# Second attention of a two-layer kernel: both maximum fills of a head ahead of the value product on TensorE

## What is computed

```python
mixed_q = hidden_states @ wq + bq
mixed_k = hidden_states @ wk + bk
mixed_v = hidden_states @ wv + bv
...                                   # P and Z, one pair for each query and head
G = -(j[None, None, None, :] - P[..., None]) ** 2 * 2.0 / Z[..., None] ** 2
scores = jnp.einsum('bhqd,bhkd->bhqk', q, k) / jnp.sqrt(jnp.float32(D))
scores = scores + G
probs = jax.nn.softmax(scores, axis=-1)
ctx = jnp.einsum('bhqk,bhkd->bhqd', probs, v)
...
return ctx @ wo + bo
```

## Time and profile before

| | us |
|---|---|
| median of 3 runs | 1796.94 |
| lowest and highest | 1796.51, 1797.92 |
| profiled execution | 1798.3 |
| span from its first to its last instruction | 1796.6 |
| first fill for the maxima starts | 1046.3 |
| last fill starts | 1726.2 |
| last scores of the stage start | 1772.1 |

### The profile page before, as it was taken

How to read it: one execution, slowest core, us unless ns; L and a number is a source line. 1 busy time by engine, 2 the same in 40 slices (tenths; PEclk the granted TensorE clock), 3 DMA queues, 4 the chain that set the end, 5 groups by cost and what they waited for, 6 DMA issues and landing times.

```text
span 1796.6 us, 27707 instructions
## 1 busy us (share of the span) xinstructions
PE 1649.1 (92%) x10488; PEld 492.0 (27%) x10488; DVE 1277.0 (71%) x2570; ACT 965.8 (54%) x1109; POOL 670.0 (37%) x408
## 2 busy tenths in 40 slices
PE   7999999999999999995999769999999999999995
PEld 3232323333333323322444311111111111111122
DVE  6767576666667575722233489999999999999974
ACT  2444545444444444442343315777777777777774
POOL 4577877878887878892000110000000000000012
PEclk8999999999999999997999857999999999999998
DMA  4100000000000000001012440111211121111000
GB/s 112 35 9 13 14 13 9 12 13 10 16 7 19 8 16 10 13 13 31 2 36 58 100 94 1 24 24 24 41 24 31 31 46 26 24 23 24 2 2 24
DMA packets 76215, 46.40 MB, mean 26 GB/s; under 512 B 22158, under 2 KB 74930, under 8 KB 76082
## 3 DMA queue, kind: packets, MB, share of 16 engines
q1 hardware_dynamic: 74738, 43.38, 11.4%
q10 hardware_dynamic: 1344, 1.25, 0.2%
HBM read 25.66 MB, written 9.31 MB: 19 GB/s over the span
## 4 chain that ended last, share of the span: by engine, by line
PE 29%; DVE 17%; ACT 3%; DMA 2%; issue 1%; SPq 1%; POOL 0%; DVEq 0%; ACTq 0%; POOLq 0%
DVE maxpart L1717 15%; PE ps_o L1613 9%; PE ps_h L1013 6%; PE ps_r L1575 5%; ACT probs L1534 3%; PE ps_e L1603 2%; DMA qrows<-maxrow 2%; PE ps_g L995 1%; PE ps_u L1000 1%; PE ps_u L1022 1%; PE ps_r L1592 1%; SPq L1456 0%; PE ps_g L1091 0%; PE ps_r L1658 0%; PE ps_j L1044 0%
## 5 line engine op out<-in xcount | busy, mean ns | idle before, releaser
L1717 DVE TENSOR_REDUCE maxpart<-ps_r 128x1 f32<-128x512 f32 x1024 | 634.5, 682 | 26.8 <-PE ps_r L1575 25.9
L1534 ACT ACTIVATE probs<-ps_e 128x1024 f32<-128x1024 f32 x512 | 504.7, 1023 | 194.9 <-PE ps_e L1603 189.8
L328 POOL TENSOR_TENSOR acc<-acc,probs 128x1024 f32<-128x1024 f32 (+3 forms) x256 | 502.9, 1964 | 77.9 <-ACT probs L362 55.3
L362 ACT ACTIVATE probs<-ps_e 128x1024 f32<-128x1024 f32 (+1 forms) x320 | 285.7, 901 | 380.7 <-DVE ps_e L697 131.0
L1575 PE MATMUL ps_r<-krows,qrows 60*128 60x512 bf16 x1024 | 346.9, 402 | 50.8 <-DVE maxpart L1717 17.9
L528 PE MATMUL ps_o<-probs,v 128*64 128x512 f32 (+3 forms) x1280 | 308.6, 561 | 0.2 <-ACT pv_raw L369 0.2
L618 DVE TENSOR_REDUCE maxpart<-ps_x 128x2 f32<-128x1024 f32 x192 | 234.5, 1222 | 75.3 <-PE ps_x L443 75.3
L1603 PE MATMUL ps_e<-qrows,krows 62*128 62x512 bf16 x1024 | 278.8, 386 | 4.2 <-DMA qrows<-maxrow 3.3
L1613 PE MATMUL ps_o<-probs,v 128*9 128x512 f32 x2048 | 269.2, 598 | 12.4 <-ACT probs L1534 12.3
L1499 POOL TENSOR_TENSOR rstd<-veps,power 128x4 f32<-128x4 f32 x8 | 8.1, 1014 | 700.2 <-DVE veps L1767 700.2
L1575 PEld LDWEIGHTS ps_r<-krows,qrows 60*128 60x128 bf16 x1024 | 80.0, 94 | 466.2 <-DVE maxpart L1717 340.4
(11 more groups left out here) (258 smaller groups left out, 1368.6 us busy)
## 6 DMA issues: line engine op xcount, KB each, us to landing
qrows<-q_rows SPq DMA_DIRECT2D x64, 192.0 KB
rbc<-rden SPq DMA_DIRECT2D x128, 64.0 KB, 2.1
q_rows<-parts_q SPq DMA_DIRECT2D x24, 128.0 KB, 2.4
k_rows<-parts_k SPq DMA_DIRECT2D x24, 128.0 KB, 2.4
krows<-k_rows SPq DMA_DIRECT2D x16, 192.0 KB, 5.9
w_rows<-parts_w SPq DMA_DIRECT2D x6, 256.0 KB, 2.6
qrows<-a_rows SPq DMA_DIRECT2D x64, 24.0 KB
qrows<-w_rows SPq DMA_DIRECT2D x64, 24.0 KB
```

The source lines that it names most:

```text
L328: pool.tensor_tensor(acc[:, u % 2, :, o:], acc[:, u % 2, :, o:], probs[:, turn % RING, :, o:], ALU.add)\
L362: act.activation(probs[:, turn % RING, :, o:], ps_e[:, turn % 2, :, o:], ACT.Exp, scale=1.0 / math.sqrt(D0))\
L1534: act.activation(probs[:, HG * (turn % 2) + hh], ps_e[:, e % 2], ACT.Exp).then_inc(s_ex, 1)
L1717: dve.reduce_max(maxpart[:, at:at + 1], ps_r[:, k, :], AX.X).then_inc(s_bf[k], 1)
```

## The change

The first two ring operations that are left in `rest` are now issued together between the scores and the value product of a head. Before, the first stood ahead of the value product and the second behind it. Heads without a value product issue the same as before.

```diff
@@ -1668,13 +1668,11 @@
                 rest, late = list(ops), turn % TU == 1
                 for hh in range(HG):
                     scores(turn, hh)
-                    for op in rest[:1]:
+                    for op in rest[:2]:
                         ring(op)
+                    rest = rest[2:]
                     if hh % 2 == late and turn > 0:
                         pv(turn - 1, hh // 2)
-                    for op in rest[1:2]:
-                        ring(op)
-                    rest = rest[2:]
                     if turn >= (NU - 1) * TU and (turn % TU, hh) in PE_SLOT:
                         step(*PE_SLOT[turn % TU, hh])
                 for op in rest:
```

## The result

The changed kernel takes 1824.82 us (median of 4 runs, 1823.66 to 1825.24) against 1797.26 for the kernel before in runs beside it (1796.51 to 1797.92). The ratio is 1.0152, with a 95% interval of 1.0135 to 1.017: slower by 27.6 us. The forecast was 1823.5.

The account below looks back on a forecast made before the run. The bound was taken as a TensorE-VectorE loop through a three-bank ring, not VectorE's busy time. Per unit 1.76 + 0.29 - 0.25 = +1.8 us, over 14.75 units +26.6: 1796.94 becomes 1823.5 us, range 1813 to 1832.

Parts of the forecast that it names:

- short interval: Steady turn, between value products, through the first fill behind one: scores now come first, 2.47 us becomes 2.69, +0.22.
- long interval: Steady turn's other gap between value products: stays 2.69 us, but set by fills waiting for reduces instead of by ScalarE.
- rest of a unit: Intervals of a unit (eight key-tile turns) outside the steady pattern, walked singly; whole unit +1.8 us.
- waits for the placed maxima: Interval between value products set by the load of the maxima: 3.29 us before and after, 0.
- six fills: Interval with six fills between value products, on the fill loop: +0.22 us.
- output turn: Interval where the second fill ahead of the second value product needs the transposes' bank: 2.65 to 2.94 us, +0.29.
- five fills: Interval with five fills between value products, on the fill loop: +0.22 us.
- maxima turn: Turn with the transposed maxima, whose first value product now waits for a reduce: 3.03 to 2.78 us, -0.25.
- rule against the row: TensorE: the row-group rule would free a slot by pairing fills; a trace row shows it already shared, so no gain.
- Faster: Rival: pairing takes TensorE out of the loop, turns fall to 4.8 us, 1753 us in all; chance 0.06.
- No change: Rival: the 0.22 us meets slack at the first fill in every short interval, 1797 us; chance 0.05.
- Slower still: Rival: the exponential's path, value product to scores to exponential, does not shorten, 13 us more, 1837 us; chance 0.05.

Follow-up runs that it names:

- experiments at one value product only: Kernel before, with the new order at only one of a turn's two value products: at the first only 1796.41 us, at the second only 1831.65 us.
- swapped fill: Changed kernel, first fill of a head following a value product placed between the two scores matmuls, which also change places: 1799.35 us, ratio 1.002.
- value product first: Against the kernel before, the value product stands directly behind its head's scores and both fills behind it: 1828.32 us, ratio 1.0174.
- late value products: Value products at heads 1 and 3 in turns 3 to 6 too: in the kernel before 1785.76 us, in the changed kernel 1816.41 us.
- fill between the scores: Changed kernel, first fill of a head following a value product placed between the two scores matmuls, these in usual order: 1821.01 us, ratio 1.0141.
- new order at the second value product: Kernel before, with both fills ahead of only the second of a turn's two value products: 1831.65 us, ratio 1.0194.

## Why the prediction was right

**The bound.** Read as a loop of two engines rather than by the busy shares. The experiments at one value product only bear this out: the same instructions with only their places changed take 1796 or 1832 us.

**The short interval, +0.22.** Predicted 2.69, measured 2.68 to 2.69. That the step between the scores and the first fill is its cause is shown by the swapped fill, which takes that step away and brings the short interval back to 2.48, and by the value product first, which puts scores on the other side of the loop and has steady turns as long, 5.39.

**The long interval, unchanged.** Predicted to change its owner from ScalarE to the fill loop at the same length. The late value products show both sides: 2.69 falls to 2.47 in the kernel before and stays 2.69 in the changed one.

**The rest of a unit.** The value products of the changed kernel, the view of the earlier trace rows:

```profile
1400.83 1.04 PE L1613 MATMUL ps_o<-probs,v 128*9 128x512 f32 x8
1404.11 1.04 PE L1613 MATMUL ps_o<-probs,v 128*9 128x512 f32 x8
1406.79 1.04 PE L1613 MATMUL ps_o<-probs,v 128*9 128x512 f32 x8
1410.67 1.05 PE L1613 MATMUL ps_o<-probs,v 128*9 128x512 f32 x8
...
1414.88 1.05 PE L1613 MATMUL ps_o<-probs,v 128*9 128x512 f32 x8
1417.83 1.05 PE L1613 MATMUL ps_o<-probs,v 128*9 128x512 f32 x8
1421.11 1.05 PE L1613 MATMUL ps_o<-probs,v 128*9 128x512 f32 x8
...
1442.59 1.04 PE L1613 MATMUL ps_o<-probs,v 128*9 128x512 f32 x8
1445.37 1.05 PE L1613 MATMUL ps_o<-probs,v 128*9 128x512 f32 x8
```

| interval | before | predicted | after |
|---|---|---|---|
| waits for the placed maxima | 3.29 | 3.29 | 3.28 |
| six fills | 3.66 | 3.88 | 3.88 |
| output turn | 2.65 | 2.94 | 2.95 |
| five fills | 3.06 | 3.28 | 3.28 |
| maxima turn | 3.03 | 2.78 | 2.78 |
| unit | 42.79 | 44.6 | 44.54 |

**The sum.** 14.75 units at +1.8 gave 26.6 us. By the measured units it is 14.75 x 1.75 = 25.8; the span grew by 1823.5 - 1796.6 = 26.9, the medians differ by 27.6. The first fill starts at 1046.7 instead of 1046.3, so 0.4 us of that lies ahead of the stage. What is left of the difference, about 1 us, is within the spread of the runs. The bounds that the prediction lists add up to 1814 and 1835, while its range ends at 1832; the upper end is 3 us short of its own terms, which the measured time did not put to the test.

**The rule against the row.** The prediction set the rule on row groups aside, since the row showed the slot shared already. That held for the sum: pairing two fills freed nothing. But which rows two neighbours work on is what makes the 0.22 at all. The prediction took the step as what two scores matmuls take together; the fill between the scores shows that one of them is enough when it is on the fill's own rows (1.20 us from the value product to the fill), and that it costs nothing when it is on the others (0.98). The size held all the same, since it was read from a row with the scores in the same order. The Trainium skill, "TensorE: Matmul & The Clock Gate", Part 3, says that matmuls in different row groups run concurrently. The trace agrees with it, 0.98 against 1.20 us.

**The rivals.** Faster: the fourth fill of each interval waits for its bank as before (the bracket at 1431.53), and the gain never came; the reason was the one given, the value product had moved behind that wait. No change: no first fill of a steady turn had slack. Slower still: the exponential's path did shorten to 2.47, which shows on its own only in the kernel with the new order at the second value product, 2.48.

## What to carry to other kernels

Where two engines hand a small ring of buffers back and forth, follow one buffer round and write the loop down as a sum; the order of two cheap instructions in it can be worth more than any engine's busy time, and half of a change can cost more than the whole. What stood directly behind the long product on the same queue decided this loop; the place belongs to the instruction that the other engine waits for. When matmuls use half of the rows, try neighbours on different halves; which half comes first was worth 22 us here.

## What the runs showed of the hardware beyond expectation

In the kernel with the fill between the scores, the instructions stand as scores, fill, scores, fill. The profile's rows start both scores together at 1432.83 and both fills together at 1433.05: by its starts the second scores matmul, on free rows, passed the fill that waited for the rows of the first. The exponential that needs it starts at 1433.50, 0.67 behind that start, where it is 0.43 in the changed kernel (1430.14 to 1430.57). So its end was told as late as if it had started beside the fill at 1433.05, 0.45 ahead of the exponential. Whether the matmul really ran early and its completion was held back in order, or only its recorded start is early, these runs don't tell.
